# Whole first loads and dummy products between the transposes, in a cross-attention kernel on one core

## What is computed

```
# block 0: channel attention both ways between x and y
res_p2r = xca(heads(x, wq_rgb), heads(y, wk_point), heads(y, wv_point)) @ proj_p2r.T
res_r2p = xca(heads(y, wq_point), heads(x, wk_rgb), heads(x, wv_rgb)) @ proj_r2p.T
x1 = (x + res_p2r + y + res_r2p)            # per batch, 128 x 1024
# block 1: channel attention of y with itself, applied to x1
q, k, v = Wq y + bq, Wk y + bk, Wv x1 + bv
attn = softmax(q k^T / sqrt(128))           # per head, over the channels of the head
o = Wo (attn v) + bo + x1
out = (o - mean(o)) / sqrt(var(o) + 1e-5) * gn_w + gn_b    # mean, var over a whole batch item
```

## Time and profile before

| | |
|---|---|
| median of three runs | 336.73 us |
| profiled execution | 336.78 us |
| its span, first to last instruction | 335.0 us |
| TensorE products busy | 322.2 us (96%) |
| TensorE weight loads busy | 268.6 us (80%) |
| VectorE busy | 261.4 us (78%) |
| ScalarE busy | 234.8 us (70%) |
| GpSimd busy | 188.3 us (56%) |
| transfers | 73.73 MB, mean 220 GB/s |

### The profile page before, as it was taken

The page is one execution under the profiler, slowest core; times in us unless marked ns, Lnnn a source line. Parts: engine busy times, 40 slices in busy tenths (PEclk is TensorE's granted clock), DMA queues, the critical chain, the costliest instruction groups (busy, mean ns, idle before and its releaser), DMA issues.

```text
span 335.0 us, 8099 instructions
## 1 busy us (share of the span) xinstructions
PE 322.2 (96%) x2566; PEld 268.6 (80%) x2566; DVE 261.4 (78%) x677; ACT 234.8 (70%) x382; POOL 188.3 (56%) x277
## 2 busy tenths in 40 slices
PE   7999999999999999999999999999999999999980
PEld 5788888897888889797888879788888978887750
DVE  2565997979698797969789796969979796983774
ACT  3646868778686877778677787867787786865332
POOL 0973892855829194673909476491928558291010
PEclk9999999999999999999999999999999999999995
DMA  7996899799696969979697978969597990203014
GB/s 233 391 287 180 239 284 280 207 305 258 204 297 175 313 161 294 247 241 286 170 302 196 274 222 270 294 168 314 168 299 178 296 268 14 112 0 127 1 58 193
DMA packets 39050, 73.73 MB, mean 220 GB/s; under 512 B 4608, under 2 KB 26368, under 8 KB 39040
## 3 DMA queue, kind: packets, MB, share of 16 engines
q1 hardware_dynamic: 35008, 58.92, 62.5%
q10 hardware_dynamic: 4032, 14.68, 12.1%
HBM read 56.81 MB, written 16.78 MB: 220 GB/s over the span
## 4 chain that ended last, share of the span: by engine, by line
PE 92%; DVE 3%; issue 2%; DMA 1%; ACT 1%; SPq 0%; POOLq 0%; POOL 0%
PE gacc L372 34%; PE oacc L392 10%; PE oacc L393 9%; PE oacc L397 9%; PE mid L482 4%; PE mid L416 4%; PE mid L459 4%; PE tpx L329 4%; PE mid L468 3%; PE mid L419 2%; PE mid L469 2%; PE mid L429 1%; DMA raw<-in_ctx 1%; PE mid L471 1%; PE mid L470 1%
## 5 line engine op out<-in xcount | busy, mean ns | idle before, releaser
L1034 POOL TENSOR_TENSOR xy_lo<-raw,xy_hi 128x256 fp32r<-128x256 f32 x256 | 177.8, 736 | 116.2 <-ACT xy_hi L642 116.2
L372 PE MATMUL gacc<-t 128*128 128x257 f32 x512 | 124.7, 385 | 0.8 <-ACT t L574 0.8
L372 PEld LDWEIGHTS gacc<-t 128*128 128x128 f32 x512 | 93.2, 190 | 15.6 <-issue 2.6
L642 ACT ACTIVATE xy_hi<-raw 128x1024 fp32r<-128x1024 f32 x64 | 67.1, 1051 | 0.0
L792 DVE STREAM_TRANSPOSE t<-y_blocks 128x512 f32<-128x512 f32 x56 | 63.9, 1141 | 0.0
L392 PE MATMUL oacc<-xy_hi,pq_hi 128*128 128x512 f32 x124 | 51.9, 418 | 0.3 <-ACT pq_hi L621 0.2
L393 PE MATMUL oacc<-xy_lo,pq_hi 128*128 128x512 f32 x124 | 49.0, 395 | 0.0
L649 ACT ACTIVATE res<-oacc 128x512 f32<-128x512 f32 x60 | 35.7, 596 | 11.4 <-PE oacc L397 9.6
L813 DVE BATCH_NORM_STATS2 hstat<-res 128x6 f32<-128x512 f32 x60 | 39.4, 677 | 1.4 <-ACT res L649 1.4
L397 PE MATMUL oacc<-xy_hi,pq_lo 128*128 128x512 f32 x124 | 38.9, 394 | 0.0
L663 ACT ACTIVATE res<-res,nbias,nscale 128x1024 f32<-128x1024 f32 x29 | 35.9, 1237 | 0.5
(11 more groups left out here) (117 smaller groups left out, 456.3 us busy)
## 6 DMA issues: line engine op xcount, KB each, us to landing
raw<-in_x SPq DMA_DIRECT2D x31, 512.0 KB, 4.4
raw<-in_ctx SPq DMA_DIRECT2D x31, 512.0 KB, 6.1
y_blocks<-in_ctx SPq DMA_DIRECT2D x112, 128.0 KB, 5.1
out<-res ACTq DMA_DIRECT2D x28, 512.0 KB, 3.5
x_blocks<-in_x SPq DMA_DIRECT2D x56, 128.0 KB, 4.9
out<-res SPq DMA_DIRECT2D x4, 512.0 KB, 2.6
wt<-in_weights SPq DMA_DIRECT2D x1, 896.0 KB, 6.8
raw<-in_x SPq DMA_DIRECT2D x2, 256.0 KB, 3.4
```

Source lines behind the costliest of these rows:

```text
L372: mm = pe.matmul(gacc[:, 0:2 * C + 1], t[slot][:, c, C:2 * C], t[slot][:, c, :], start=(c == 0), stop=(c == CH - 1))
L642: act.activation(xy_hi[slot][:, s, :], raw[slot][:, s, :], ACT.Copy).then_inc(split_hi, 1)
L1034: piece = pool.tensor_tensor(xy_lo[slot][:, s, cols], raw[slot][:, s, cols], xy_hi[slot][:, s, cols].bitcast(f32), ALU.subtract)
```

## The change

x0 and y0 are no longer loaded in halves: the order is x0, y0, x1, y1, each in one transfer, and the semaphores for the halves and the two memsets go. WARM is 3, and the dummy products write to `gacc` in place of `oacc`. TensorE transposes both halves of x0, runs three dummy products, and then transposes both halves of y0; before, halves of x0 and y0 alternated.

```diff
-WARM = 2
+WARM = 3
...
-            for i in range(2):
-                cols = slice(HALF * i, HALF * (i + 1))
-                sp.dma_start(raw[0][:, 0, cols], x[0][:, cols]).then_inc(x_half_in[i], 16)
-                sp.dma_start(raw[0][:, 1, cols], y[0][:, cols]).then_inc(y_half_in[i], 16)
-            load_x(0, 1)
-            load_y(0, 1)
+            for n in range(2):
+                load_x(0, n)
+                load_y(0, n)
...
-            def warm_up():
+            def warm_up(count):
-                for k in range(WARM):
-                    pe.matmul(oacc[0][:, 0:3 * C], warm[:, 0:C], warm[:, C:4 * C], start=True, stop=True)
+                for k in range(count):
+                    pe.matmul(gacc[:, 0:3 * C], warm[:, 0:C], warm[:, C:4 * C], start=True, stop=True)
...
-            warm_up()
+            warm_up(WARM)
...
             def x_transpose_early(n, i):
-                if n == 0:
-                    pe.wait_ge(x_half_in[i], 16)
-                elif i == 0:
+                if i == 0:
                     pe.wait_ge(x_in[n], 16)
...
             def y_transpose_early(n, i):
-                if n == 0:
-                    pe.wait_ge(y_half_in[i], 16)
-                elif i == 0:
+                if i == 0:
                     pe.wait_ge(y_in[n], 16)
...
                     x_transpose_early(0, 0)
+                    x_transpose_early(0, 1)
+                    warm_up(3)
                     y_transpose_early(0, 0)
-                    x_transpose_early(0, 1)
                     y_transpose_early(0, 1)
                     gram_chunks(h, u, 0, 0, 4)
...
                 act.wait_ge((x_in, y_in)[s][slot], 16 * (h + 1))
-                if isinstance(n, int) and n == 0:
-                    for half in range(2):
-                        act.wait_ge((x_half_in, y_half_in)[s][half], 16)
...
-            dve.memset(gate[:, 8:9], 0.0).then_inc(x_in[0], 16)
-            dve.memset(gate[:, 9:10], 0.0).then_inc(y_in[0], 16)
```

More of the change, by code:

```diff
@@ L99, in cross_attention_pair_kernel @@
         pq_lo = [sb(f"pq_lo{n}", [C, 2, 2, C], f32r) for n in range(2)]
-        gate = sb("gate", [1, 10])
+        gate = sb("gate", [1, 8])
         hstat = sb("hstat", [C, 2, 2, 6])
@@ L132, in cross_attention_pair_kernel @@
         x_blocks_in = [sem(f"x_blocks_in{n}") for n in range(2)]
-        x_half_in = [sem(f"x_half_in{n}") for n in range(2)]
-        y_half_in = [sem(f"y_half_in{n}") for n in range(2)]
         stored = [sem(f"stored{n}") for n in range(4)]
```

## The result

The changed kernel takes 338.98 us in the median of 14 runs (338.0 to 340.2 us), the kernel before 337.49 us in 14 runs beside them (336.71 to 338.48 us). The ratio is 1.0046 with an interval of 1.0031 to 1.0061: slower by 1.5 us. The time lies in the forecast range and on the forecast side, but the difference is little more than half of the +2.65 us that the sum gave (56%). The profiled executions differ by more than the medians: 339.56 us after, 336.78 us before, +2.78 us.

The account below looks back on a forecast made before the run. TensorE, busy 96% of the span, was taken as the bound; profiled 336.78 us plus 2.65 us of later Gram start gave 339.43 us, stated as 339.4 us, range 337.8 to 340.6 us.

Parts of the forecast that it names:

- the sum: Whole run: profiled 336.78 us before plus 2.65 us of later first Gram product gives 339.43 us.
- What bounds the kernel: Whole span: TensorE is the bound, computing 322.2 of 335.0 us, so opening delays carry through one for one.
- the loop is paced by its loads: Rival, behind the opening: waits on transfers swallow the late opening, 335.8 to 336.8 us; chance 0.04.
- The new order, step by step: Opening until the first Gram product: its start moves from 7.95 to 10.60 us, +2.65 us.
- The landings: Opening loads: x0 there at 4.5 to 5.6 us, y0 at 5.7 to 7.4 us, no wait taken.
- y0's upper bound: Opening load of y0: landed by 7.4 us at the latest, when its second half landed before.
- early rise: Rival, opening: TensorE's full clock comes sooner through three opening products; 337.6 to 338.7 us, chance 0.22.
- the dummies hiding nothing: Between x0's and y0's transposes: three dummy calls cost 1.95 us, ending 1.7 us or more after y0's landing.
- The median of the runs, 336.73 us, is 0.05 us off that: Starting point: median before agrees with the profiled 336.78 us, so the forecast was put at 339.4 us.
- in the trace the work from 1.47 to 5.25 us had not raised it: Opening, argument against the early rise: the transpose group from 5.64 us was still slow.
- late rise: Rival, opening: x0's transposes keep the clock low until the dummies end; +4.55 us, 341.3 us, chance 0.07.
- Part regained: Rival, idle gap before 14.25 us: the 0.83 us closes, leaving +1.8 us, 338.6 us; chance 0.07.

Follow-up runs that it names:

- only the loads whole: Changed kernel with two opening dummy products, transposes in the order of before, no products between: 338.07 us, ratio 1.0006 to the kernel before.
- without products between: Changed kernel without the three dummy products between the transposes of x0 and y0: 337.51 us, ratio 0.9996 to the kernel before.
- two opening products: Changed kernel with two opening dummy products in place of three, the three between kept: 338.79 us, ratio 1.0030 to the kernel before.
- before, three opening: Kernel before with three opening dummy products in place of two: 337.11 us, ratio 0.9979 to the kernel before.
- before, gap filled: Kernel before with one 128-column dummy product between the transposes of x0's and y0's first halves: 336.85 us, ratio 0.9987 to the kernel before.
- before, both: Kernel before with three opening dummy products and one 128-column dummy product between x0's and y0's first-half transposes: 337.28 us, ratio 0.9989.
- transposes between: Changed kernel with 18 transposes of the zeroed tile replacing the three dummy products between: 339.56 us, ratio 1.0036 to the kernel before.
- six products between: Changed kernel with six dummy products between x0's and y0's transposes in place of three: 340.89 us, ratio 1.0091 to the kernel before.

## Right and wrong, point by point

**What bounds the kernel: right, and tighter than claimed.** Take from each trace the end of the first eight Gram instructions in the chain, and its span (the rise, read from the distances between the starts of TensorE's instructions, is used further down; all in us):

```
trace                      rise           end of Gram half 1   span    difference
before                     7.1                   9.86          335.0      325.1
before, second trace       9.9                  11.31          336.2      324.9
before, third trace       13.0                  13.15          338.1      325.0
after                      7.1                  12.61          337.8      325.2
after, second trace        4.4                  11.95          336.8      324.9
after, third trace         4.4                  11.77          336.7      324.9
only the loads whole       in a wait, by 4.8    11.83          336.7      324.9
without products between   4.6                   9.87          334.8      324.9
two opening products      10.6                  14.11          339.1      325.0
before, three opening      in a wait, by 7.0    11.00          335.9      324.9
before, gap filled         6.9                  10.02          335.0      325.0
before, both               7.3                  10.54          335.5      325.0
transposes between         7.6                  12.86          337.8      324.9
six products between       6.8                  14.40          339.6      325.2
```

Over 4.5 us of shift the rest stays within 0.3 us. Everything that the change does to the time, it does ahead of the ninth Gram instruction, to within these 0.3 us, and "the loop is paced by its loads" is ruled out.

**The new order, step by step: right** for a rise at 7.1 us: 10.60 us forecast, 10.63 us in the trace; span +2.8 us.

**The landings: right for x0, wrong for y0's upper bound.** x0 landed at 4.5 us (3.3 us after its issue; 4.5 to 5.6 us forecast), and inside that range in the other traces with whole loads. y0 landed at 7.48 us against 7.4 us as the upper bound, and at 6.2 to 8.3 us in the eight traces with whole loads, behind the bound in four. I had bounded a landing from one trace; it moves by 2 us from execution to execution. With the early rise the 8.1 us did set the start, where the sum had the dummies hiding nothing.

**The step that was wrong inside a forecast that held: "The median of the runs, 336.73 us, is 0.05 us off that".** I took the agreement of one trace and three runs for proof that the trace of before is typical. It is one of its best: of the 14 runs in the result four took less than 337 us. The rise at 7.1 us was put down as the place of the clock in this kernel, and the spread of 1.0 us in three runs as a possible price of before in the chances. It belonged in the sum. The medians give the account: before lies 0.71 us above its trace (337.49 against 336.78 us), after 0.58 us below its own (338.98 against 339.56 us), and 2.78 - 0.71 - 0.58 = 1.49 us, the measured difference. This only says where the difference sits; what moves executions of one kernel is the rise and the landings, as the traces show. That the forecast of 339.4 us came within 0.45 us of 338.98 us is in part luck: its base was 0.76 us too low (336.73 against 337.49 us) and its step 1.16 us too high (+2.65 against +1.49 us), and the two errors have opposite signs.

**The rivals.** The early rise, given 0.22, is what happened in two of three traces of the changed kernel; of its range, 337.6 to 338.7 us, one trace (338.5 us) lies inside and one (338.94 us) 0.2 us above; its Gram products start at 9.97 us, just above the 9.9 us of the range's upper edge, and the rest lies outside its span (2.1 us in place of 1.8 us). The argument against it, "in the trace the work from 1.47 to 5.25 us had not raised it", was read off a single execution of the kernel before. The trace with only the loads whole has the same two opening products and had risen by 4.8 us. The late rise was not seen in the changed kernel, but in the variant with two opening products, at its price. "Part regained" is wrong: the gap of 0.83 us is in every trace. What I left out is what the dummies could be for: without them TensorE waits for y0, and a wait may cost clock. If they guard against that, the guard costs 1.7 us here, and its gain can't be seen in the times: without them the ratio is 0.9996.

**What stays open.** That idle time in the opening delays the rise or lets the clock fall is argued, not proved. For it: the three latest rises (9.9, 10.6 and 13.0 us) are in the three traces where TensorE had waited 0.6 us or more (0.61, 0.64 and 1.62 us) before the rise; where it had waited less or not at all, the rise came by 7.6 us; the one fall came behind a wait of 1.45 us; and the third opening product made the kernel before faster. But idle time is not the whole of it. The changed kernel's three traces have no idle time between the first product and the rise, and it came at 7.1, 4.4 and 4.4 us; and up to 4.2 us all fourteen traces have the same four dummy instructions at the same pace. So something that differs from execution to execution, whatever the kernel, moves the rise by nearly 3 us, and it could stand behind a part of the other differences too. No run here tells the two apart, nor how much idle time it takes, nor why the landings differ.

## What to carry to other kernels

Where an engine is busy 96% of the span, an edit of the opening costs its price one for one (here the rest stayed within 0.3 us over 4.5 us of shift); but the opening's own length varies with the clock's rise and the landings, so trace both kernels several times before taking a single trace as the place where a sum starts. Dummy products in an opening are to be measured and not assumed: a third opening product with half transfers gave 0.9979, a short filler in a wait 0.9987 with an interval that includes 1, and 1.95 us of products at a place where the wait is mostly over cost 1.7 of their 1.95 us.

## What the hardware showed that was not expected

- The clock's rise came in the opening products at 4.4 us, at 7.1 us, at about 9.9 us and at about 13 us, in executions with the same first 4 us; and in one, after a rise and a wait of 1.45 us, the granted clock fell to 0.50 for over 3 us.
- The column of the granted clock reads 1.00 ahead of its first recorded change, also where the rows go at half pace; the distance between starts tells the clock (0.64 against 0.32 us for 384 columns).
- y0, one transfer of 0.5 MB issued at 1.68 us, landed at 6.2 to 8.3 us in eight executions with the same transfers ahead of it.
